# Deeper buffers, sums of the values three steps on, and an expert's transfers in two steps of four

## The chip, the cores and the metric

The kernel runs on one core of one Trainium2 chip. The metric is the device time of one execution in microseconds (us), as the median of the runs. Five engines work side by side, each through its own list of instructions in order, and wait for one another with semaphores: TensorE (PE, matmuls, with weight loads as PEld), VectorE (DVE), ScalarE (ACT), GpSimd (POOL) and SyncE (SP, which here only issues transfers). Transfers run on 16 DMA engines that all issuers share.

## The reference

Two transformer layers on 16 sequences of 112 tokens, width 256, each with a context of 375 rows. Layer A: cross-attention with 8 heads of 64, then a mixture of 8 experts of which each token takes two. Layer B: cross-attention with 16 heads, then a feed-forward part with a convolution and quantised weights. Cut to what matters here:

```python
sim  = einsum('bqhd,bkhd->bhqk', q * SCALE, k)      # keys: 375 context rows + 112 latents = 487
attn = softmax(where(valid, sim, NEG_INF))
out  = einsum('bhqk,bkhd->bqhd', attn, v) @ Wout
x    = x + tanh(g_xattn[0]) * out
# experts: h = silu(x @ w1[e].T) * (x @ w3[e].T);  y = h @ w2[e].T;  8 experts, top 2 by a router
```

All products are made to nearly f32 precision by splitting each operand into two f16 halves (high and low) and adding three products (`PASSES`).

## The kernel before

**Steps and pairs.** The attention work is cut into 192 pairs of heads: 64 pairs in layer A (four of each sequence), then 128 in layer B (eight of each). All engines walk the same list of steps `j` from -9 on, each with its own code for the step. In step `j` PE makes the scores of pair `j`, the queries and keys of pair `j + 2`, the values of pair `j`, and then, in `sum_values(j - 2)`, the product of probabilities and values of pair `j - 2`. A head of a pair is a unit `u = 2 * j + h`.

**The way of one unit.** PE writes the scores; DVE masks them and finds the minimum (`mask_scores`, L1438); ACT takes the exponential (`exp`, L927) and rounds to f16 (`round_probs`, L934) into buffer `u % 4` of `PR`; POOL subtracts to get the low half (`split_probs`, L711); SP issues a DMA transpose (`turn_probs`, L569) of the 112 x 1024 f16 values into buffer `u % 5` of `PT`; PE sums (`sum_values`, L1190: per head 12 matmuls of 64 columns). A buffer of `PR` is free when the transpose of unit `u - 4` has landed, a buffer of `PT` when unit `u - 5` is summed. The values of a pair are in `vN`, two buffers by `j % 2`: ACT rounds pair `j`'s values (`round_v`, L954) in step `j`, after the sum of pair `j - 2`. PE waits in `sum_values` for the values' split, for the transpose, and, in the first unit of eight, for `norm_out` of the group of eight before (L1470), which DVE does in step `4 * g + 6`.

**The experts' weights.** Beside the first steps ACT and DVE turn the f32 weights of the eight experts into f16 halves: three chunks of 512 columns in two steps (`expert_chunks`), so one expert (six chunks) in four steps. ACT issues its plain transfers in `load_weights(j)`, after `round_probs`: for expert `e` three loads of a third (128 partitions x 1024 f32, 512 KB each) from HBM into `raw`, which hold the weights of the expert two before until they are split; and three stores of f16 halves, 512 KB each, back to HBM. In every four steps ACT also loads one context (375 KB, L853), at the head of a step `4 * k + 2`, and spills one turned context (375 KB, L858), at the head of a step `4 * k`. From step 38 on, the tokens of the first six sequences run through the experts (`up`, `down`), with weights and rows that SP loads.

**Order around the change.** Per step ACT does `round_q`, `exp` twice, `round_k`, `round_probs` twice, `load_weights`, `round_v`, context and latents, `round_expert`. The rounding of layer B's weights (`round_l1_chunk`) goes one chunk a step from step 49 on into `W`; chunks 17 and 19 to 23 of `W` are written last.

## Time and profile before

| | |
|---|---|
| runs | 1463.2, 1463.97, 1465.99 us, median 1463.97 |
| profiled execution | 1468.41 us, of which the span from first to last instruction is 1466.7 us |
| mean granted TensorE clock | 0.956 |
| PE, DVE, ACT, POOL busy | 86%, 73%, 66%, 75% of the span |
| DMA | 239.99 MB, mean 164 GB/s |

The span is what the rows are measured in; "busy" is an average over stages with different limits.

### The profile page before, as it was taken

How to read it: one execution, taken by the hardware profiler on the slowest of the kernel's cores; microseconds unless marked ns; L12 is line 12 of the kernel's file. 1: busy time of each engine (PE TensorE's matmuls, PEld its weight loads, DVE VectorE, ACT ScalarE, POOL GpSimd, SP SyncE). 2: the span in 40 equal slices, each digit the busy share in tenths (PEclk: the TensorE clock that was granted, in tenths of full speed). 3: DMA queues.
4: the chain of work that ended last, by engine and by line, in shares of the span. 5: the costliest groups of instructions: out<-in, count | busy, mean ns of one | idle time of the engine just before them, and what ended most of it. 6: DMA issues, size and time to landing. Idle time of an engine off the chain costs nothing.

```text
span 1466.7 us, 45534 instructions
## 1 busy us (share of the span) xinstructions
PE 1256.6 (86%) x16920; PEld 983.7 (67%) x16920; DVE 1066.3 (73%) x2851; ACT 971.8 (66%) x2319; POOL 1094.1 (75%) x1346
## 2 busy tenths in 40 slices
PE   1877788779899988868999999999999999999863
PEld 1555566558777766646888788677777777777652
DVE  5788677966566678775666666778878778888655
ACT  2887778656556666544656465777787877787741
POOL 5887777687677765464777767798888888889763
PEclk9999889989999999998999999999999999999995
DMA  7799998799999968458999999456454545445420
GB/s 252 160 205 192 203 202 169 126 213 236 233 244 269 261 137 200 102 116 198 246 253 247 238 259 224 95 105 111 94 101 99 105 104 100 100 94 103 79 64 7
DMA packets 453500, 239.99 MB, mean 164 GB/s; under 512 B 390320, under 2 KB 424992, under 8 KB 452768
## 3 DMA queue, kind: packets, MB, share of 16 engines
q1 hardware_dynamic: 417912, 178.51, 62.5%
q10 hardware_dynamic: 32296, 51.23, 11.7%
q0 software_dynamic: 3072, 7.34, 1.7%
q8 instruction: 135, 2.21, 0.7%
q14 instruction: 85, 0.70, 0.2%
HBM read 107.78 MB, written 35.50 MB: 98 GB/s over the span
## 4 chain that ended last, share of the span: by engine, by line
PE 52%; POOL 12%; ACT 10%; DMA 7%; DVE 7%; issue 7%; DVEq 2%; ACTq 2%; another core or an unknown queue 0%; SPq 0%; POOLq 0%
PE bank_ring L1171 10%; PE bank_ring L1157 9%; PE bank_ring L1209 8%; PE bank_scores L1131 5%; PE bank_out L1190 5%; DMA probs_turned<-probs 4%; PE bank_x L1272 4%; PE bank_x L1223 4%; POOL probs L711 3%; PE bank_x L1144 3%; ACT scores L927 3%; ACT probs L934 2%; DVE scores L1438 2%; ACTq L1072 2%; POOL moe_rows L730 1%
## 5 line engine op out<-in xcount | busy, mean ns | idle before, releaser
L711 POOL TENSOR_TENSOR probs<-scores,probs 112x487 f16<-112x487 f32 x373 | 414.1, 1127 | 203.9 <-ACT probs L934 199.1
L927 ACT ACTIVATE scores<-scores,score_min 112x487 f32<-112x487 f32 x384 | 265.9, 694 | 159.1 <-DVE score_min L1438 157.0
L1438 DVE CUSTOM_DVE_ANT_0 scores<-bank_scores,mask 112x487 f32<-112x487 f32 x384 | 238.2, 657 | 1.8 <-PE bank_scores L1131 1.3
L934 ACT ACTIVATE probs<-scores 112x487 f16<-112x487 f32 x384 | 214.3, 604 | 32.2 <-DMA probs_turned<-probs 16.5
L1190 PE MATMUL bank_out<-values,probs_turned 128*128 128x64 f16 x4608 | 172.7, 195 | 40.5 <-DMA probs_turned<-probs 21.8
L1171 PE MATMUL bank_ring<-weights,kv_B 128*128 128x128 f16 x3072 | 195.4, 220 | 5.6 <-DVE keys L1455 3.9
L1171 PEld LDWEIGHTS bank_ring<-weights,kv_B 128*128 128x128 f16 x3072 | 184.0, 99 | 15.3 <-DVE keys L1455 5.2
L954 ACT ACTIVATE values<-bank_ring 128x512 f16<-128x512 f32 x192 | 112.3, 585 | 119.5 <-PE bank_out L1190 111.2
L1190 PEld LDWEIGHTS bank_out<-values,probs_turned 128*128 128x128 f16 x4608 | 158.7, 99 | 46.4 <-issue 25.3
L1460 DVE SCALAR_TENSOR_TENSOR values<-bank_ring,values 128x512 f16<-128x512 f32 x192 | 132.2, 688 | 77.3 <-ACT values L954 73.1
L1157 PE MATMUL bank_ring<-kv_B,weights 128*128 128x488 f16 x768 | 180.3, 371 | 0.0
L1131 PE MATMUL bank_scores<-keys,queries 64*112 64x488 f16 x1152 | 164.6, 392 | 4.1 <-DVE score_min L1438 3.7
L1209 PE MATMUL bank_ring<-raw_weights,expert_up 128*128 128x128 f16 x2064 | 131.2, 221 | 13.8 <-issue 13.8
L1209 PEld LDWEIGHTS bank_ring<-raw_weights,expert_up 128*128 128x128 f16 x2064 | 122.9, 99 | 26.0 <-issue 18.4
L1455 DVE SCALAR_TENSOR_TENSOR keys<-bank_ring,keys 128x488 f16<-128x488 f32 x192 | 126.1, 657 | 10.7 <-ACT keys L947 5.3
L947 ACT ACTIVATE keys<-bank_ring 128x488 f16<-128x488 f32 x192 | 106.6, 555 | 4.0 <-PE bank_ring L1157 3.7
L1171 PE MATMUL bank_ring<-weights,kv_A 128*128 128x128 f16 x1536 | 101.9, 226 | 6.6 <-DVE keys L1455 6.6
L1157 PEld LDWEIGHTS bank_ring<-kv_B,weights 128*128 128x128 f16 x768 | 69.4, 99 | 56.2 <-issue 1.7
L1171 PEld LDWEIGHTS bank_ring<-weights,kv_A 128*128 128x128 f16 x1536 | 96.1, 102 | 11.8 <-DVE keys L1455 8.0
L940 ACT ACTIVATE queries<-bank_x 128x112 f16<-128x112 f32 x192 | 49.2, 256 | 75.0 <-PE bank_x L1144 69.4
L1157 PE MATMUL bank_ring<-kv_A,weights 128*128 128x488 f16 x384 | 98.6, 397 | 0.0
L1131 PEld LDWEIGHTS bank_scores<-keys,queries 64*112 64x112 f16 x1152 | 61.1, 129 | 41.3 <-issue 15.0
(236 smaller groups left out, 2446.0 us busy)
## 6 DMA issues: line engine op xcount, KB each, us to landing
expert_up<-experts_up SPq DMA_DIRECT2D x86, 512.0 KB, 5.3
expert_down<-experts_down SPq DMA_DIRECT2D x43, 512.0 KB, 5.7
raw_weights<-in_weights ACTq DMA_DIRECT2D x18, 512.0 KB, 6.7
experts_up<-expert_up ACTq DMA_DIRECT2D x16, 512.0 KB, 4.6
probs_turned<-probs SPq DMA_TRANSPOSE x384
context_turned_B<-kv_B ACTq DMA_DIRECT2D x16, 375.0 KB, 8.0
kv_B<-context_turned_B ACTq DMA_DIRECT2D x16, 375.0 KB, 4.0
moe_results<-moe_result SPq DMA_DIRECT2D x43, 128.0 KB, 5.3
```

Source lines behind the costliest of these rows:

```text
L711: pool.tensor_tensor(PR[:, u % 4, 1, 0:KEYS], S[:, u % 4, 0:KEYS], PR[:, u % 4, 0, 0:KEYS], ALU.subtract).then_inc(probs_split[u % 2], 1)
L927: act_e.activation(S[:, u % 4, 0:KEYS], S[:, u % 4, 0:KEYS], ACT.Exp, bias=rmin[:, u % 4:u % 4 + 1], scale=-1.0, accum_out=rsum[:, g % 2, ...
L934: act_e.activation(PR[:, u % 4, 0, 0:KEYS], S[:, u % 4, 0:KEYS], ACT.Copy).then_inc(probs_ready, 1)
L954: act_e.activation(vN[:, j % 2, 0], bank("v", j)[:].rearrange("p (t d) -> p t d", t=4), ACT.Copy, scale=1 / WSCALE).then_inc(v_hi, 1)
L1131: last = pe.matmul(bS[h][0:TOK, 0:KW], qT[r, j % 2, a, :], kT[r, j % 2, b, :], start=n == 0, stop=n == 2)
L1157: last = pe.matmul(bK[:, 0:KW], w(wk + kb * step, a, 128 * (j % 4), 128), kv[layer][:, n % 2, kb, b, 0:KW], start=i == 0, stop=i == 5)
L1171: last = pe.matmul(bV[:, 128 * t:128 * t + 128], kv[layer][:, n % 2, kb, a, 128 * t:128 * t + 128], w(wv + kb * step, b, 128 * (j % 4), 12 ...
L1190: last = pe.matmul(bO[:, col:col + HD], PT[u % PT_BUFS][:, at:at + 128], vN[:, j % 2, b, t, HD * h:HD * h + HD], start=i == 0, stop=i == 11)
L1209: last = pe.matmul(bH[:, 128 * q:128 * q + 128], eup[:, t % 2, at:at + 128], xT[:, t % 2, KB * c + kb, :], start=k == 0, stop=k == 5)
L1438: dve.tensor_tensor_reduce(out=S[:, u % 4, 0:KEYS], in0=bS[u % 2][0:TOK, 0:KEYS], in1=mask[:, m, 0:KEYS], scale=1.0, scalar=3.0e38, op0=AL ...
L1455: dve.scalar_tensor_tensor(kT[:, j % 2, 1, :], bank("k", j)[:, 0:KW], 1 / WSCALE, kT[:, j % 2, 0, :], ALU.mult, ALU.subtract).then_inc(k_s ...
L1460: dve.scalar_tensor_tensor(vN[:, j % 2, 1].rearrange("p t d -> p (t d)"), bank("v", j)[:], 1 / WSCALE, vN[:, j % 2, 0].rearrange("p t d -> ...
```

## The change

It has these parts.

1. `PT` has 8 buffers, `PR` 6 and `vN` 3 for the first 56 pairs, then 5, 4 and 2 as before. The added ones lie in chunks 17 and 19 to 23 of `W`. `in_turn` makes a table of (buffer, the user before it, how many uses) for every unit or pair. `round_l1_chunk(10)`, the first that writes into one of these chunks, waits for the sum of pair 55.
2. `summed_in(j)`: pairs up to 51 are summed three steps on, except that the last pair of a sequence (`p % 4 == 3`) is still summed two steps on. So a step `4 * k + 1` sums two pairs, a step `4 * k + 2` none. From pair 52 on all are summed two steps on.
3. `expert_loads` and `expert_stores`: counted in fours, loads of the thirds go from steps 0, 1, 3 to steps 1, 1, 2, and stores from 1, 2, 3 to 1, 2, 2. All six plain transfers of a cycle are issued in steps `4 * k + 1` and `4 * k + 2`.
4. Where `split_probs` of the second head goes from POOL to DVE and back (steps 33 to 37 and 73 to 78), the first waits for the split before it instead of for its transpose.
5. DVE sets the pads of the added buffers to zero at the start: four more small `memset`s.

```diff
-PT_BUFS = 5
+LONG_PAIRS = 56
+PT_BUFS, PR_BUFS, V_BUFS = (8, 5), (6, 4), (3, 2)
+def summed_in(j):
+    return [p for p in (j - 3, j - 2) if is_pair(p) and j - p == (3 if p < LONG_PAIRS - 4 and p % 4 < 3 else 2)]
+def in_turn(count, long_count, bufs):
+    places, last, uses = [], {}, {}
+    for i in range(count):
+        b = i % (bufs[0] if i < long_count else bufs[1])
+        uses[b] = uses.get(b, 0) + 1
+        places.append((b, last.get(b), uses[b]))
+        last[b] = i
+    return places
+PT_AT = in_turn(2 * PAIRS, 2 * LONG_PAIRS, PT_BUFS)
+PR_AT = in_turn(2 * PAIRS, 2 * LONG_PAIRS, PR_BUFS)
+V_AT = in_turn(PAIRS, LONG_PAIRS, V_BUFS)
 def expert_loads(j):
-    return [(e, p) for e in range(2, EXPERTS) for p in range(3) if j == 4 * (e - 2) + (4, 5, 7)[p]]
+    return [(e, p) for e in range(2, EXPERTS) for p in range(3) if j == 4 * (e - 2) + (5, 5, 6)[p]]
 def expert_stores(j):
-    return [(e, p) for e in range(EXPERTS) for p in range(3) if j == 4 * e + 5 + p]
+    return [(e, p) for e in range(EXPERTS) for p in range(3) if j == 4 * e + (5, 6, 6)[p]]
...
             def turn_probs(u):
-                if u >= PT_BUFS:
-                    sp.wait_ge(values_summed, u - PT_BUFS + 1)
+                buf, prev, _ = PT_AT[u]
+                if prev is not None:
+                    sp.wait_ge(values_summed, prev + 1)
...
             def round_l1_chunk(c):
                 act_e.wait_ge(l1_loaded[c % len(L1_SLOTS)], 16 * (c // len(L1_SLOTS) + 1))
+                if c == 10:
+                    act_e.wait_ge(values_summed, 2 * LONG_PAIRS)
...
             def round_probs(u):
-                if u >= 4:
-                    act_e.wait_ge(turned[(u - 4) % PT_BUFS], turns_done(u - 4))
+                prev = PR_AT[u][1]
+                if prev is not None:
+                    act_e.wait_ge(turned[PT_AT[prev][0]], turns_done(prev))
...
             def round_v(j):
                 act_e.wait_ge(v_ready, j + 1)
-                if j >= 2:
-                    act_e.wait_ge(values_summed, 2 * (j - 1))
+                prev = V_AT[j][1]
+                if prev is not None:
+                    act_e.wait_ge(values_summed, 2 * prev + 2)
...
                 expert(m[1])
-                if is_pair(j - 2):
-                    sum_values(j - 2)
+                for p in summed_in(j):
+                    sum_values(p)
...
                     if any(j == steps[0] for steps in VECTOR_SPLITS):
-                        dve.wait_ge(turned[(2 * j - 1) % PT_BUFS], turns_done(2 * j - 1))
+                        dve.wait_ge(probs_split[1], j)
                     split_probs(2 * j + 1)
```

## Rows read from the trace of the kernel before

**Rows 1.** The page: busy time by engine, and DMA share in 40 slices.

```profile
PE 1256.6 (86%) x16920; PEld 983.7 (67%) x16920; DVE 1066.3 (73%) x2851; ACT 971.8 (66%) x2319; POOL 1094.1 (75%) x1346
...
DMA  7799998799999968458999999456454545445420
```

**Rows 2.** Four-step stretches: length, PE, PEld, DVE, ACT, POOL busy, PEclk, DMA share, GB/s.

```profile
62.30:91.60 29.30, 21.13 (x278) 15.33 (x279) 24.13 (x60) 24.58 (x57) 24.34 (x28) 0.94 0.97 169
91.60:118.90 27.30, 23.10 (x295) 16.86 (x294) 22.84 (x57) 22.61 (x53) 22.92 (x31) 0.94 1.12 217
118.90:150.60 31.70, 23.92 (x296) 17.47 (x295) 23.02 (x58) 22.99 (x53) 23.03 (x31) 0.89 1.13 191
150.60:180.20 29.60, 23.67 (x295) 17.43 (x295) 22.59 (x58) 22.73 (x53) 22.87 (x31) 0.90 1.13 197
180.20:210.10 29.90, 24.25 (x297) 17.62 (x296) 22.56 (x58) 22.80 (x53) 22.88 (x31) 0.90 1.08 196
...
241.20:266.10 24.90, 20.23 (x283) 14.73 (x282) 22.29 (x63) 20.22 (x48) 21.69 (x29) 1.00 0.85 167
...
424.60:463.70 39.10, 37.59 (x538) 31.68 (x536) 27.02 (x70) 25.43 (x61) 30.09 (x46) 1.00 1.15 268
```

**Rows 3.** The chain that ended last, from 120 us: start, us, what.

```profile
135.42 13.70 DMA probs_turned<-probs
...
150.70 1.40 PE bank_scores L1131 x6
...
158.18 0.76 PE bank_scores L1131 x6
...
159.34 1.24 PE bank_ring L1157 x6
...
182.36 2.26 PE bank_ring L1157 x6
...
196.87 11.70 DMA probs_turned<-probs
```

**Rows 4.** Waits of PE from 39.2 to 210.1 us: total, times, longest.

```profile
PE bank_out L1190 <- DMA probs_turned<-probs: 21.8, 9, 4.2
PE bank_out L1190 <- issue: 4.8, 4, 1.2
```

**Rows 5.** PE in order of time, 60 to 96 us; idle before in brackets.

```profile
61.53 0.52 PE L1190 MATMUL bank_out<-values,probs_turned 128*128 128x64 f16 x12 [0.66 <-DMA probs_turned<-probs]
...
91.10 0.52 PE L1190 MATMUL bank_out<-values,probs_turned 128*128 128x64 f16 x12 [3.36 <-DMA probs_turned<-probs]
```

**Rows 6.** ACT in order of time, 150 to 181 us; idle before in brackets.

```profile
157.92 0.60 ACT L954 ACTIVATE values<-bank_ring 128x512 f16<-128x512 f32 x1 [1.64 <-PE bank_out L1190]
...
166.61 0.70 ACT L927 ACTIVATE scores<-scores,score_min 112x487 f32<-112x487 f32 x1 [0.66 <-DVE score_min L1438]
...
178.73 0.61 ACT L934 ACTIVATE probs<-scores 112x487 f16<-112x487 f32 x1 [3.23 <-DMA probs_turned<-probs]
```

**Rows 7.** DMA queues, 118 to 151 us: packets, MB, share of 16 engines.

```profile
q1 hardware_dynamic: 9528, 2.37, 70.3%
q10 hardware_dynamic: 1792, 4.00, 41.9%
```

**Rows 8.** DMA queue of SP, 596 to 625 us: eight transposes, hardly anything else.

```profile
q1 hardware_dynamic: 7424, 1.84, 29.5%
```

**Rows 9.** Short stretches, columns as in rows 2.

```profile
136.00:148.00 12.00, 5.90 (x84) 4.35 (x84) 8.85 (x20) 7.76 (x18) 7.68 (x9) 0.95 1.33 132
...
131.00:132.30 1.30, 1.30 (x17) 0.69 (x14) 1.30 (x3) 1.22 (x5) 0.80 (x1) 1.00 0.05 13
...
180.00:182.00 2.00, 2.00 (x13) 1.05 (x14) 1.14 (x3) 2.00 (x4) 1.92 (x3) 0.50 1.14 340
```

**Rows 10.** DVE in order of time, 0 to 30 us.

```profile
1.08 0.13 DVE L1378 MEMSET probs_turned<- 128x8 uint32 x5
...
6.58 1.08 DVE L1484 BATCH_NORM_STATS2 bn_stats<-context 125x6 f32<-125x256 f32 x3 [2.11 <-DMA context<-in_ctx]
```

More of the change, by code:

```diff
@@ L349, in build @@
         PR = sb("probs", [TOK, 4, 2, 512], F16)
-        PT = [sb(f"probs_turned_{i}", [128, 8 * TOK + 16], F16) for i in range(PT_BUFS)]
+        PT = [sb(f"probs_turned_{i}", [128, 8 * TOK + 16], F16) for i in range(PT_BUFS[1])]
+        PT += [W[:, 2 * c * CHUNK:2 * c * CHUNK + 8 * TOK + 16] for c in (23, 19, 17)]
+        PR_more = W[0:TOK, 2 * 20 * CHUNK:2 * 22 * CHUNK].rearrange("p (b a c) -> p b a c", b=2, a=2)
+        vN_more = W[:, 2 * 22 * CHUNK:2 * 23 * CHUNK].rearrange("p (a t d) -> p a t d", a=2, t=4)
         mask = sb("mask", [TOK, 2, KEYS + 1], BF16)
@@ L443, in build @@
         probs_ready, probs_split = sem("probs_ready"), [sem("probs_split_0"), sem("probs_split_1")]
-        turned = [sem(f"probs_turned_{i}") for i in range(PT_BUFS)]
+        turned = [sem(f"probs_turned_{i}") for i in range(PT_BUFS[0])]
         values_summed, out_normed, o_hi = sem("values_summed"), sem("out_normed"), sem("o_hi")
@@ L501, in turns_done, with probs, values @@
         def turns_done(u):
-            return 16 * (u // PT_BUFS + 1)
+            return 16 * PT_AT[u][2]
+        def probs(u):
+            b = PR_AT[u][0]
+            return PR[:, b] if b < PR_BUFS[1] else PR_more[:, b - PR_BUFS[1]]
+        def values(j):
+            b = V_AT[j][0]
+            return vN[:, b] if b < V_BUFS[1] else vN_more
         block = stack.enter_context(nc.Block())
@@ L568, in turn_probs @@
                 sp.wait_ge(probs_split[u % 2], u // 2 + 1)
-                sp.dma_start_transpose(PT[u % PT_BUFS][:, 0:8 * TOK].rearrange("p (j q) -> p j q", j=8),
-                                       PR[:, u % 4].rearrange("p a c -> p (a c)"))\
-                    .then_inc(turned[u % PT_BUFS], 16)
+                sp.dma_start_transpose(PT[buf][:, 0:8 * TOK].rearrange("p (j q) -> p j q", j=8),
+                                       probs(u).rearrange("p a c -> p (a c)"))\
+                    .then_inc(turned[buf], 16)
             for j in STEPS:
@@ L710, in split_probs @@
                 pool.wait_ge(probs_ready, u + 1)
-                pool.tensor_tensor(PR[:, u % 4, 1, 0:KEYS], S[:, u % 4, 0:KEYS],
-                                   PR[:, u % 4, 0, 0:KEYS], ALU.subtract).then_inc(probs_split[u % 2], 1)
+                pool.tensor_tensor(probs(u)[:, 1, 0:KEYS], S[:, u % 4, 0:KEYS],
+                                   probs(u)[:, 0, 0:KEYS], ALU.subtract).then_inc(probs_split[u % 2], 1)
             def split_hidden(b, i, half):
@@ L824, in _ @@
                     if any(j == steps[-1] + 1 for steps in VECTOR_SPLITS):
-                        pool.wait_ge(turned[(2 * j - 1) % PT_BUFS], turns_done(2 * j - 1))
+                        pool.wait_ge(probs_split[1], j)
                     split_probs(2 * j + 1)
@@ L931, in round_probs @@
             def round_probs(u):
-                if u >= 4:
-                    act_e.wait_ge(turned[(u - 4) % PT_BUFS], turns_done(u - 4))
-                act_e.activation(PR[:, u % 4, 0, 0:KEYS], S[:, u % 4, 0:KEYS], ACT.Copy).then_inc(probs_ready, 1)
+                prev = PR_AT[u][1]
+                if prev is not None:
+                    act_e.wait_ge(turned[PT_AT[prev][0]], turns_done(prev))
+                act_e.activation(probs(u)[:, 0, 0:KEYS], S[:, u % 4, 0:KEYS], ACT.Copy).then_inc(probs_ready, 1)
             def round_q(j):
@@ L951, in round_v @@
                 act_e.wait_ge(v_ready, j + 1)
-                if j >= 2:
-                    act_e.wait_ge(values_summed, 2 * (j - 1))
-                act_e.activation(vN[:, j % 2, 0], bank("v", j)[:].rearrange("p (t d) -> p t d", t=4), ACT.Copy,
+                prev = V_AT[j][1]
+                if prev is not None:
+                    act_e.wait_ge(values_summed, 2 * prev + 2)
+                act_e.activation(values(j)[:, 0], bank("v", j)[:].rearrange("p (t d) -> p t d", t=4), ACT.Copy,
                                  scale=1 / WSCALE).then_inc(v_hi, 1)
@@ L1183, in sum_values @@
                         pe.wait_ge(out_normed, u // 8)
-                    pe.wait_ge(turned[u % PT_BUFS], turns_done(u))
+                    pe.wait_ge(turned[PT_AT[u][0]], turns_done(u))
                     i = 0
@@ L1189, in sum_values @@
                             at = TOK * (4 * a + t)
-                            last = pe.matmul(bO[:, col:col + HD], PT[u % PT_BUFS][:, at:at + 128],
-                                             vN[:, j % 2, b, t, HD * h:HD * h + HD], start=i == 0, stop=i == 11)
+                            last = pe.matmul(bO[:, col:col + HD], PT[PT_AT[u][0]][:, at:at + 128],
+                                             values(j)[:, b, t, HD * h:HD * h + HD], start=i == 0, stop=i == 11)
                             i += 1
@@ L1376, in _ @@
             dve.memset(PR[:, :, :, KEYS:512], 0.0)
+            dve.memset(PR_more[:, :, :, KEYS:512], 0.0)
             for t in PT:
@@ L1444, in split_probs @@
                 dve.wait_ge(probs_ready, u + 1)
[L1445 removed]
+                dve.tensor_tensor(probs(u)[:, 1, 0:KEYS], S[:, u % 4, 0:KEYS], probs(u)[:, 0, 0:KEYS],
                                   ALU.subtract).then_inc(probs_split[u % 2], 1)
```

5 lines of the change are left out of this document (2 added, 3 removed).

## The prediction

> **What bounds the kernel now.** I read the page first, for the whole: PE is busy 86% of the span, and the DMA engines stand near full in the first half and near half in the second [rows 1]. The change touches layer A up to pair 55, so I cut that part into stretches of four steps, one sequence each, and read busy time, clock and DMA share in each [rows 2]. Three kinds of stretch show. From 62 to 210 us (steps 4 to 23) four steps take 27.3 to 31.7 us while no engine is busy for more than 24.6, and the DMA share is 0.97 to 1.13 (it passes 1 since packets of two queues overlap). From 241 us, where the experts' loads are over, four steps take 24.9 us. In the stage with the experts' products, as at 424 us, PE is busy 37.6 of 39.1 us at full clock.
>
> Then the chain of waits [rows 3]. From step 4 to 23 it runs on PE alone, broken once in four steps by a DMA transpose that took 11.7 to 13.7 us from issue to landing (three such from 135 us). PE waited 21.8 us for transposes between 39 and 210 us [rows 4]; these waits stand in steps 3, 7, 11, 15, 19 and 23, always for pair `4k + 1`; those of steps 3 and 7 are 0.7 and 3.4 us [rows 5]. The same list over the whole run gives the same line, so no later stage has such a wait. So 21.8 us is the prize, plus what follows from it: after each wait the granted clock is 0.50, the lower of the two levels (1.2 of 2.4 GHz), where before it was 1.00 [rows 9], and the same six score matmuls take 1.40 in place of 0.76 us, the six key matmuls 2.26 in place of 1.24 us [rows 3]. These two alone are 1.66 us a wait.
>
> **The change, part by part.**
>
> *Sums three steps on.* Pair `4k + 1` is now due one step, some 6 us, later. The longest waits were 4.2 us for one head, some 4.5 for the pair, so at today's landing times each would go: 21.8 us for six waits, 1.66 us of clock for each of the last five, 8.3 us. One more wait goes: PE waited four times up to 1.2 us for `norm_out` before the first sum of a group (4.8 us in all, [rows 4]); that sum moves one step behind `norm_out`. PE's own limit on this change is therefore about 21.8 + 8.3 + 4.8 = 34.9 us.
>
> *ACT.* ACT waited 3.2 us per cycle for a transpose to free a buffer of `PR` [rows 6]; with six buffers it waits for one a pair older, so this goes too. It is not on the chain by itself, but it held the next `exp` and the transfers behind it. ACT's other waits in such a cycle are 1.64 us for the sum before `round_v` and 0.66 us for masked scores [rows 6]. The first stays, since the third buffer of `vN` comes with a sum one step later, except in one step of four. ACT is busy 22.7 to 23.0 us per four steps [rows 2]; with 2.3 to 2.6 us of such waits it can't do a cycle under about 25.3 us. DVE and POOL, at 22.6 to 23.0, say the same, and the cycle at 241 us took 24.9. I take 25.3 us as the engines' floor.
>
> *DMA.* This is where I doubt that the whole prize comes. Four steps move 5.8 MB (197 GB/s x 29.6 us). Eight transposes with hardly anything beside them take 29.5% of 29 us, 8.6 us of the DMA engines [rows 8]. In the stretch from 118 to 151 us the same queue moved 2.37 MB, which at that rate is 11.1 us, but took 70.3% of 33 us, 23.2 us; the plain queue took 13.8 us for 4.00 MB [rows 7]. So transposes beside plain transfers cost twice their time, and from 136 to 148 us the two together moved 132 GB/s [rows 9]. The DMA engines idle only while PE's wait starves the issuers: 131.0 to 132.3 us at a share of 0.05 [rows 9]; I estimate 1.0 us of such idle time per cycle from this one of 1.3. If the transfers stay as inefficient, a cycle can't fall under 29.6 (the mean of the four from 91 to 210 us, [rows 2]) - 1.0 = 28.6 us, whatever the buffers.
>
> *Grouping the six transfers.* Before, every pair's transposes meet a plain transfer: ACT issues them in all four steps. After, 3.1 MB plus the context (0.38 MB) go out within about 6 us, and the transposes of two pairs of four (`4k + 1`, `4k + 2`) meet them, both with three steps to land. Pairs `4k + 3` and `4k` meet only the spill and the tail of the group. What this saves isn't shown by any row. Below: nothing, 28.6 us a cycle. Above: all transposes clean, 8.6 + 13.8 = 22.4 us, and then the engines' floor of 25.3 counts. I take the middle, 27.0 us, since about half of the transposes still meet plain transfers.
>
> A rule of the Trainium skill speaks against any saving here: "DMA: Bandwidth & Descriptors", section Queues, rings and completion order, has each DMA engine take turns between the queues it has work for, packet by packet; by that alone the order of transfers moves no work, and a cycle stays at 28.6 us. The share of 70.3% against 29.5% says that taking turns isn't all that happens beside transposes.
>
> *The sum.* By stretches of [rows 2]: 27.3 to 27.0 saves 0.3; 31.7, 29.6 and 29.9 to 27.0 save 10.2; the one at 62 us, with a DMA share under 1, loses its wait of 3.4 us; the short wait in step 3 gives 0.7. Together 14.6 us. The waits for `norm_out` and the clock are inside these cycles and aren't added. Against it I set 1.5 us for steps 24 to 36, where pair `4k + 3` is now the only one with two steps and meets stores gathered just before it. Net 13.1 us.
>
> *Edits costed at nothing.* The steps from 38 to 55 are bound by PE (37.6 of 39.1 us busy), and the same matmuls stay; if that cover were gone, earlier transposes could only help. A sum moved within a cycle is 0.7 us of PE work in another place. The wait in `round_l1_chunk(10)` is for a sum made two steps before. Dropping POOL's or DVE's wait for a transpose at steps 33, 38, 73 and 79 takes away a wait that isn't on the chain; with the cover gone it would be worth at most a landing, 3 us each. Four more memsets, like the five that took 0.13 us together, lie ahead of a context load that DVE waits for 2.1 us [rows 10]; uncovered they would cost some 0.1 to 0.5 us. `load_weights` issues the same transfers, none with a new wait that ACT meets: each load waits for a split at least a step old.
>
> The profiled execution took 1468.4 us, 1.7 more than its span, so after the change it should show 1455.3, with a span of 1453.6. The median of the runs is 4.4 us lower, so 1463.97 - 13.1 = 1450.9 us; I say 1451.
>
> **The rivals.**
>
> *The engines' floor is reached.* If grouping makes the transposes nearly clean, four cycles of 25.3 us save 2.0 + 6.4 + 4.3 + 4.6 = 17.3, with the 4.1 of steps 3 and 7 and none lost: 21.4 us, 1442.6 us. For it: 22.4 us of clean DMA work in a cycle. Against: two pairs still meet 3.5 MB.
>
> *Grouping saves nothing.* Cycles of 28.6: 3.1 + 1.0 + 1.3 + 4.1 = 9.5, less 1.5: 8.0 us, 1456.0 us. This is also what the skill's rule gives.
>
> *The wait moves and stays.* Pair `4k + 3` has its two steps still, and its transposes stand behind those of pair `4k + 2` in SP's queue, which now meet the group. If PE waits there as long as it did for `4k + 1`, the cycle stays near 29.6 us, and the time near 1463, within 3 us.
>
> *Slower.* The same place at a higher price. The group, a context and four transposes are 3.15 + 0.38 + 0.92 = 4.45 MB; the other four transposes take 4.3 us clean. A cycle of 29.6 us leaves 25.3 us for the 4.45 MB, 176 GB/s. Under that rate the change is slower than before. The stretch at 136 us had 132 GB/s, whole cycles have 191 to 217. At 160 GB/s a cycle takes 32.1 us, 2.5 longer, over six cycles with loads 15 us: 1479 us.
>
> **How the numbers follow.** A measurement of this kernel tells about 0.2% (3 us) from no change. Chances: the middle case with its neighbours (1446 to 1455) 0.42; the floor 0.12; grouping saves nothing or part of the wait stays (1455 to 1461) 0.19; the wait moves whole 0.14; slower 0.13. That makes faster 0.73, same 0.14, slower 0.13. The likeliest case's own range is 1445 to 1457. For 8 in 10 the range runs from the engines' floor, 1441, to no change and a little over, 1466.
>
> **What would show it.** Right: PE waits for transposes before step 24 fall from 21.8 us to under 8; four steps there take 26 to 28 us; the clock in these stretches rises from 0.90; the DMA share stays near 1 with more GB/s. Steps from 24 on keep their lengths within 1 us each. Grouping right: the share of SP's queue for the same MB falls. Wrong: waits of PE for transposes in steps `4k + 1` from 5 on (the wait moved), or ACT or DVE late in the cycle with PE waiting for masked scores or keys (the floor lies higher than 25.3), or a slower start of steps 24 to 37.

## The result and the profile after

The changed kernel takes 1473.87 us, the median of 7 runs (1470.09 to 1482.97), against 1463.97 us of 7 runs before. The ratio is 1.0087, with a 95% interval from 1.0054 to 1.0120: the change makes the kernel slower, by 9.9 us going by the medians and by some 13 us going by the ratio. I had said 1451.

The profiled execution took 1477.87 us with a span of 1476.1, 9.4 more than before. Single executions differ more than I knew when I predicted. The kernel before ran from 1446 to 1478 us in the comparisons below, and its first profile, at 1468.4, lies high. So I profiled each kernel twice; the second profile of the kernel before took 1452.7 us, that of the changed kernel 1467.6. Where two numbers stand for these two kernels, as 147.8 / 138.1, they are of the first and the second profile.

The page, PE and the DMA engines in 40 slices, against [rows 1]:

```profile
PE 1265.4 (86%) x16920; PEld 991.4 (67%) x16920; DVE 1060.0 (72%) x2855; ACT 970.0 (66%) x2319; POOL 1093.7 (74%) x1346
...
DMA  8699999799999979358999999446354555445420
```

PE is busy 8.8 us longer with the same 16920 matmuls. That is the clock, as the stretches of four steps show. They start at step 4 and have the columns of [rows 2]: length, PE, PEld, DVE, ACT, POOL, PEclk, DMA share, GB/s.

```profile
63.00:89.30 26.30, 22.15 (x278) 16.00 (x278) 21.29 (x57) 23.40 (x56) 22.29 (x27) 0.87 0.82 160
89.30:121.30 32.00, 26.08 (x296) 18.37 (x296) 20.92 (x55) 21.71 (x50) 22.67 (x30) 0.84 1.17 175
121.30:151.60 30.30, 24.91 (x297) 18.18 (x296) 23.60 (x63) 24.42 (x58) 21.55 (x30) 0.89 1.19 184
151.60:183.80 32.20, 25.29 (x297) 18.03 (x296) 20.52 (x56) 21.18 (x49) 22.47 (x30) 0.84 1.19 200
183.80:213.20 29.40, 24.58 (x297) 17.74 (x296) 23.90 (x64) 24.46 (x58) 22.24 (x30) 0.88 1.19 200
...
244.00:268.90 24.90, 20.28 (x283) 14.65 (x282) 22.55 (x65) 20.22 (x49) 22.71 (x30) 1.00 1.00 170
431.30:470.00 38.70, 37.25 (x537) 31.62 (x534) 26.96 (x70) 25.30 (x61) 29.95 (x46) 1.00 1.15 274
```

The first stretch is 3 us shorter than its counterpart, as I expected. It is also the one in which the loads have hardly begun. The four loaded ones take 31.0 us on average, where they took 29.6 before and I had forecast 27.0. Their DMA share rose to 1.17 to 1.19, and yet fewer bytes move in a microsecond: 190 GB/s over steps 8 to 23 against 200. The DMA engines don't idle meanwhile. In the packets' records, cut into slices of a quarter microsecond, SP's or ACT's queue fills more than 10% of the 16 engines in every slice of steps 8 to 23 of the first profile, and in all but 1.25 us of the second; in the kernel before 4 us are left empty. The clock is lower, not higher. The two stretches at the end are as before.

PE's waits from 40.2 to 213.2 us, against [rows 4]:

```profile
PE bank_out L1229 <- DMA probs_turned<-probs: 6.8, 2, 5.3
PE bank_x L1183 <- DVE router_logits L1764: 5.2, 3, 2.4
PE bank_x L1295 <- DVE moe_in_f L1761: 5.2, 3, 2.4
PE bank_out L1229 <- DMA probs_turned<-weights: 3.9, 2, 3.7
...
PE bank_out L1229 <- DMA weights<-probs: 1.3, 1, 1.3
```

(The added buffers lie in the tile `weights`, so a transpose that uses one carries that name.) The waits for transposes did fall, from 21.8 us to 12.0 (13.1 to 9.0 in the second profiles). But they fell behind a third step and not because the transposes came sooner. The chain, against [rows 3], has three transposes that took 16 to 21 us from issue to landing, where before they took 12 to 14:

```profile
82.24 16.48 DMA probs_turned<-weights
...
143.39 21.02 DMA probs_turned<-probs
...
202.27 19.23 DMA probs_turned<-probs
```

The second of them ends at 164.4 us. It releases PE, against [rows 5], and ACT, against [rows 6], at once:

```profile
164.46 0.82 PE L1229 MATMUL bank_out<-values,probs_turned 128*128 128x64 f16 x12 [5.32 <-DMA probs_turned<-probs]
```

```profile
ACT probs L972 <- DMA probs_turned<-probs: 7.0, 1, 7.0
```

The wait of ACT for a buffer of `PR` is back, longer than the 3.2 us of [rows 6], with six buffers in place of four. It comes less often: over steps 4 to 23 these waits are 10.4 / 7.3 us, where they were 15.7 / 6.1. PE's clock behind it is the lower of its levels, as in [rows 9]:

```profile
164.40:166.40 2.00, 1.95 (x19) 1.44 (x21) 0.41 (x1) 1.64 (x4) 1.25 (x2) 0.50 1.25 210
```

The DMA queues from 121 to 151 us, against [rows 7], and SP's from 602 to 632 us, where there is hardly anything else, against [rows 8]:

```profile
q1 hardware_dynamic: 6713, 1.67, 63.5%
q10 hardware_dynamic: 1749, 3.88, 53.9%
```

```profile
q1 hardware_dynamic: 7568, 1.97, 29.4%
```

The plain queue takes 53.9% of 30 us, 16.2 us, for 3.88 MB, where it took 13.8 us for 4.00 MB. The transposes take 11.4 us per MB here; before they took 9.8, and clean ones take 4.5. Per byte the packets of both kinds took longer. This is not yet engine time that is lost: it is the sum of the packets' durations, and packets of one queue overlap in the records, as the 126.9% of SP's queue alone shows further down.

After step 24 there is more. Steps 24 to 43 take 179.9 / 180.0 us, where they took 174.6 / 173.4. Steps 44 to 55 give 1 to 2 us of it back, with 117.8 / 118.5 against 120.0 / 119.6.

### The profile page after: what moved, and what is told of

The parts are those of the page before. It is cut to its first block, busy times and chain, and to the rows that moved or that the text cites. A ratio compares the mean times of both kernels' runs of the same rounds, so it can differ in the third digit from the quotient of the medians.

```text
span 1476.1 us, 45538 instructions
## 1 busy us (share of the span) xinstructions
PE 1265.4 (86%) x16920; PEld 991.4 (67%) x16920; DVE 1060.0 (72%) x2855; ACT 970.0 (66%) x2319; POOL 1093.7 (74%) x1346
## 4 chain that ended last, share of the span: by engine, by line
PE 47%; ACT 12%; POOL 10%; issue 9%; DVE 9%; DMA 8%; ACTq 3%; DVEq 2%; SPq 1%; POOLq 0%
PE bank_ring L1210 8%; PE bank_ring L1196 8%; PE bank_ring L1248 8%; PE bank_out L1229 5%; PE bank_scores L1170 5%; ACT scores L964 4%; PE bank_x L1311 3%; PE bank_x L1262 3%; DMA probs_turned<-probs 3%; PE bank_x L1183 2%; POOL probs L746 2%; DVE scores L1478 2%; ACT probs L972 2%; ACTq L1111 2%; ACT keys L985 2%
## 5 line engine op out<-in xcount | busy, mean ns | idle before, releaser
L746 POOL TENSOR_TENSOR probs<-scores,probs 112x487 f16<-112x487 f32 x338 | 373.0, 1121 | 181.5 <-ACT probs L972 179.0
L972 ACT ACTIVATE probs<-scores 112x487 f16<-112x487 f32 x348 | 193.8, 604 | 25.9 <-DMA probs_turned<-probs 11.7
L1210 PEld LDWEIGHTS bank_ring<-weights,kv_B 128*128 128x128 f16 x3072 | 184.5, 99 | 12.7 <-DVE keys L1495 4.1
L1196 PE MATMUL bank_ring<-kv_B,weights 128*128 128x488 f16 x768 | 184.0, 377 | 0.0
L1500 DVE SCALAR_TENSOR_TENSOR values<-bank_ring,values 128x512 f16<-128x512 f32 x174 | 119.8, 688 | 75.5 <-ACT values L993 71.9
L1229 PE MATMUL bank_out<-values,probs_turned 128*128 128x64 f16 x3828 | 140.7, 194 | 20.3 <-issue 10.3
L993 ACT ACTIVATE values<-bank_ring 128x512 f16<-128x512 f32 x174 | 101.4, 583 | 85.3 <-PE bank_out L1229 84.3
L1229 PEld LDWEIGHTS bank_out<-values,probs_turned 128*128 128x128 f16 x3828 | 130.3, 99 | 23.8 <-issue 12.5
L1248 PEld LDWEIGHTS bank_ring<-raw_weights,expert_up 128*128 128x128 f16 x2064 | 124.8, 100 | 25.3 <-issue 17.3
L1210 PE MATMUL bank_ring<-weights,kv_A 128*128 128x128 f16 x1536 | 105.5, 230 | 7.1 <-DVE keys L1495 7.0
L1210 PEld LDWEIGHTS bank_ring<-weights,kv_A 128*128 128x128 f16 x1536 | 99.5, 104 | 13.0 <-DVE keys L1495 9.0
```

The source lines that it names most:

```text
L746: pool.tensor_tensor(probs(u)[:, 1, 0:KEYS], S[:, u % 4, 0:KEYS], probs(u)[:, 0, 0:KEYS], ALU.subtract).then_inc(probs_split[u % 2], 1)
L972: act_e.activation(probs(u)[:, 0, 0:KEYS], S[:, u % 4, 0:KEYS], ACT.Copy).then_inc(probs_ready, 1)
L1196: last = pe.matmul(bK[:, 0:KW], w(wk + kb * step, a, 128 * (j % 4), 128), kv[layer][:, n % 2, kb, b, 0:KW], start=i == 0, stop=i == 5)
L1210: last = pe.matmul(bV[:, 128 * t:128 * t + 128], kv[layer][:, n % 2, kb, a, 128 * t:128 * t + 128], w(wv + kb * step, b, 128 * (j % 4), 12 ...
L1229: last = pe.matmul(bO[:, col:col + HD], PT[PT_AT[u][0]][:, at:at + 128], values(j)[:, b, t, HD * h:HD * h + HD], start=i == 0, stop=i == 11)
L1248: last = pe.matmul(bH[:, 128 * q:128 * q + 128], eup[:, t % 2, at:at + 128], xT[:, t % 2, KB * c + kb, :], start=k == 0, stop=k == 5)
```

## The experiments

Ratios are to the kernel before, run beside each on the same chip (its medians there were 1458.4, 1459.6 and 1459.6 us, and 1463.97 beside the changed kernel). The table has what the profiles show of each: the length of steps 4 to 23, of 24 to 43 and of 24 to 55, the DMA share and rate over steps 8 to 23, and "both", the part of steps 8 to 23 in which transposes and plain transfers are on the DMA engines together. I worked out "both" from the trace's records of packets: it is the sum of the slices of a quarter microsecond in which SP's queue and ACT's queue each fill more than 10% of the 16 engines.

| kernel | ratio (95%) | steps 4–23 | 24–43 | 24–55 | share, GB/s | both |
|---|---|---|---|---|---|---|
| before | 1 | 147.8 / 138.1 | 174.6 / 173.4 | 294.6 / 293.0 | 1.11, 200 / 1.11, 212 | 41 / 44 |
| changed | 1.0087 (1.0054–1.0120) | 150.2 / 144.2 | 179.9 / 180.0 | 297.7 / 298.6 | 1.18, 190 / 1.16, 196 | 74 / 65 |
| e1 changed, not grouped | 0.9987 (0.9951–1.0023) | 132.2 | 177.6 | 300.9 | 1.14, 220 | 40 |
| e2 before, grouped | 1.0329 (1.0280–1.0377) | 182.9 | 176.5 | 296.8 | 0.87, 159 | 60 |
| e3 deep buffers alone | 0.9968 (0.9935–1.0001) | 136.8 | 168.9 | 295.8 | 1.10, 213 | 38 |
| e4 changed, thin loads | 0.9966 (0.9932–1.0001) | 133.5 | 178.2 | 298.3 | 0.86, 173 | 21 |
| e5 changed, sums two on | 1.0285 (1.0229–1.0340) | 184.0 | 170.9 | 294.7 | 0.96, 162 | 70 |
| e6 transposes held back | 1.0103 (1.0067–1.0140) | 148.3 | 179.1 | 297.7 | 1.14, 189 | 74 |
| e7 before, thin loads | 0.9889 (0.9834–0.9944) | 130.0 | 169.3 | 286.9 | 0.92, 171 | 23 |
| e8 three steps on early only, not grouped | 0.9937 (0.9908–0.9967) | 139.8 | 168.0 | 293.3 | 1.10, 211 | 46 |
| e9 only loads grouped | 1.0176 (1.0126–1.0226) | 162.8 | 186.4 | 307.5 | 1.18, 169 | 100 |
| e10 only stores grouped | 1.0047 (1.0013–1.0081) | 144.7 | 180.1 | 298.2 | 1.12, 197 | 56 |

**e1: the change without the grouping.**

```
-    ... if j == 4 * (e - 2) + (5, 5, 6)[p]]
+    ... if j == 4 * (e - 2) + (4, 5, 7)[p]]
-    ... if j == 4 * e + (5, 6, 6)[p]]
+    ... if j == 4 * e + 5 + p]
```

> The changed kernel with the six plain transfers of a cycle back in their old steps (loads 0, 1, 3, stores 1, 2, 3), all else as changed. Theory G (grouping makes transposes and plain transfers share the DMA engines for longer, 16 to 21 us a cycle against 9 to 11 before): cycles of steps 8 to 23 fall from 30 to 32 us to about 27 to 28, mixed time falls back near 10 us, and the kernel is 8 to 14 us faster than before, near 1455. Theory B (the deeper buffers themselves let more transposes meet the plain transfers, whatever the steps): cycles stay at 30 to 32 us and the kernel is within 3 us of the changed one, near 1473. If ScalarE's running ahead is what delays the last scatters at step 38, that part (about 4 us) stays here in either case.

Its ratio is 0.9987: all that the change loses, it loses by the grouping. The same buffers and sums with it are 1.0% slower, some 15 us. Theory G holds in the cycles, which fall to 26.8 us on average, but only half in the time: 1455.7 us is near the 1455 that it names, yet the kernel before took 1458.4 beside it, so the gain of 8 to 14 us isn't there. Steps 8 to 23:

```profile
88.80:195.90 107.10, 89.54 (x1179) 66.81 (x1178) 89.42 (x229) 89.37 (x208) 93.85 (x119) 0.94 1.14 220
```

The same transfers in other steps reach 220 GB/s in place of 190, and the clock 0.94 in place of 0.86. Since the DMA engines hardly idle in either kernel (0.25 us are empty here) and the bytes are the same, the order alone changes what they move in a microsecond. PE waits for transposes only twice in steps 4 to 23, both times in step 9, for the two heads of pair 7 (`4k + 3`):

```profile
PE bank_out L1229 <- DMA weights<-probs: 7.1, 2, 5.6
```

**e2: the grouping alone, in the kernel before.** The same two lines changed the other way, with five, four and two buffers and the sums two steps on.

> The kernel before with only the six plain transfers gathered in two steps; old buffers, sums two steps on. Theory G: four transposes meet 3.5 MB of plain transfers with only two steps to land, so TensorE waits more than before: 5 to 15 us slower than before, near 1474. Theory B: grouping is harmless, within 3 us of before.

It takes 1503.48 us, 3.3% more, three times the most that I had set for theory G. PE's waits from 62.1 to 244.0 us:

```profile
PE bank_out L1190 <- DMA probs_turned<-probs: 48.7, 10, 10.4
PE bank_out L1190 <- issue: 8.2, 4, 2.1
```

With 21.1 / 12.7 us before in steps 4 to 23, the grouping adds 28 to 36 us of waiting for transposes. The mean clock over these steps falls from 0.91 to 0.82.

**e3: the deep buffers alone.** The sums are two steps on and the transfers in their old steps.

```
-    ... j - p == (3 if p < LONG_PAIRS - 4 and p % 4 < 3 else 2)]
+    ... j - p == 2]
```

> Deeper buffers only: sums two steps on for all pairs, transfers in their old steps. Theory G: TensorE's waits for pair 4k+1 stay (21.8 us before) but ScalarE's 3.2 us per cycle for a buffer of PR go, so 0 to 4 us faster than before. Theory B: as slow as the changed kernel, 5 to 10 us slower than before.

The ratio is 0.9968 (0.9935 to 1.0001), within the 0 to 4 us of theory G and just short of a difference that can be told. PE still waits 13 us for transposes in steps 4 to 23 (21.1 / 12.7 in the kernel before), ACT no longer for a buffer of `PR`.

**e4: the changed kernel with thin loads.** Each load of a third brings 128 columns in place of 1024, for experts 2 to 7, so seven eighths of these loads are left out; what is left and the stores stay grouped.

```
-    act_e.dma_start(raw[..., (2 * p + 2) * CHUNK], weights_in[:, at:at + 2 * CHUNK])
+    act_e.dma_start(raw[..., 2 * p * CHUNK + 128], weights_in[:, at:at + 128])
```

> The changed kernel with each load of a third of an expert's weights (experts 2 to 7) cut from 1024 to 128 columns, so 1.4 of 3.1 MB of a cycle's plain transfers are left out; the experts' products then use other weights, with the same work. If the DMA engines set the length of steps 4 to 27, the cycles fall to the engines' floor (I reckoned 25.3 us) and the kernel ends 20 to 35 us under the changed one, 1440 to 1453. If engines' own couplings set it, the cycles stay above 28 us and it gains under 10 us.

No wait for a transpose is left, yet the time falls only to 1455.11 us, 2 us above the range that I had set for DMA as the limit. PE's waits from 60 to 190 us:

```profile
PE bank_x L1183 <- POOL mask L735: 6.0, 3, 3.1
PE bank_x L1183 <- DVE router_logits L1764: 5.3, 3, 2.6
PE bank_x L1295 <- DVE moe_in_f L1761: 5.2, 2, 2.6
```

So this is close to the engines' own floor in the changed order (stores and contexts are still moved): 133.5 us for twenty steps, 26.7 a cycle.

**e5: the changed kernel with all sums two steps on.** The edit of e3, with the grouping kept.

> The changed kernel with its deep buffers and its grouped loads and stores, but with every sum two steps after its pair, as in the kernel before. Grouping alone, with the old buffers and sums two steps on, took 1503 us; the changed kernel, with both, 1474. Theory B (the deep buffers rescue most of it: what grouping delays is then only the pair's own transposes, and not ACT's and SP's queue behind them): 1474 to 1485 us, PE's waits for transposes between 10 and 30 us over steps 3 to 23. Theory S (the third step is what covers the transposes that meet the group, since they take 12 to 21 us from issue to landing in the changed kernel): 1490 us or more, with PE waits for transposes of 35 to 50 us. In both, steps 24 to 40 take about 131 us as in the two kernels with sums two steps on, and not 135 to 136, if it is the sums' place that lengthens those steps.

It takes 1500.84 us (1.0285), hardly less than e2. So theory S holds: with the grouping the buffers do nearly nothing, and the third step makes up for most of it. PE's waits for transposes, of 49 us in steps 4 to 23:

```profile
PE bank_out L1229 <- DMA probs_turned<-probs: 27.3, 6, 6.5
PE bank_out L1229 <- DMA probs_turned<-weights: 21.9, 4, 7.6
```

**e6: transposes held back until loads have landed.** Two waits more in SP's queue.

```
+    for e in range(2, EXPERTS):
+        for p, step in ((1, 6), (2, 7)):
+            if j == 4 * (e - 2) + step:
+                sp.wait_ge(third_loaded[e % 2][p], 16 * (e // 2))
```

> The changed kernel with two waits more in SP's queue for each expert from 2 to 7: the transposes of step 4k + 2 are issued only after the load of the second third has landed, those of step 4k + 3 only after the load of the last third has. So the transposes meet fewer plain transfers, and nothing else is changed. Theory M (a transpose beside a plain transfer costs the DMA engines about twice its time, so that what is mixed is lost): the time in which both queues are active falls from 16 to 21 us a cycle, DMA shares fall under 1.1, and the time comes at 1460 to 1468 us, 6 us or more under the changed kernel. Rival Q (the engines only take turns and no work is lost; the transposes are late because they queue behind or beside the group): transposes start later and land no earlier, the time is 1474 us or more, with PE waits for transposes of 20 us or more.

The ratio is 1.0103, within the interval of the changed kernel's own. The time fits neither theory's range (1460 to 1468, and 1474 or more). And the profile shows that the experiment missed its aim: the time in which both queues are active is 74 us, as without the waits, since the transposes of pair `4k + 1`, which meet the whole group, aren't held back by them, nor do they keep the stores away. So it can't tell one theory from the other.

**e7: the kernel before with thin loads.** The edit of e4 in the old order.

> The kernel before with the loads of the experts' thirds cut from 1024 to 128 columns (experts 2 to 7; the output is computed with other weights). The changed kernel with the same cut took 1455 us, with no PE wait for a transpose and cycles of 24.0 to 29.4 us (mean 26.7) in steps 4 to 20. If buffers and later sums are worth something once the plain transfers are gone, this one is slower than that. Theory F (the sums' place three steps on costs DVE and PE some microseconds of its own, and the old order has no waits left once transposes are clean): 1445 to 1453 us, cycles of 24 to 26 us in steps 4 to 20. Rival (the old buffers bind also without plain transfers): 1455 to 1462 us, with PE or ACT waits for transposes left in these cycles.

1440.43 us, 5 us under the range of theory F. The rival fails, and what theory F said of the cycles and waits holds: the cycles in steps 4 to 23 take 26.0 us on average, and no wait for a transpose is left but a short one. PE's waits from 60 to 190 us:

```profile
PE bank_x L1144 <- POOL mask L700: 7.7, 3, 3.8
PE bank_x L1144 <- DVE router_logits L1724: 6.4, 3, 2.3
...
PE bank_out L1190 <- DMA probs_turned<-probs: 0.3, 1, 0.3
```

Two things follow. Seven eighths of the loads cost the kernel before 1.1% (16 us; 19 by the medians), so that is about all there was to win by hiding transposes. And the changed order with the same thin loads (e4) is 0.8% slower than the old order, by 3.5 us in steps 4 to 23 and 11.4 in steps 24 to 55: even if the grouping had made all transposes clean, I estimate from e4 that the change as made would have come to about 1455 us.

**e8: deep buffers, transfers in their old steps, three steps on only for pairs before 20.**

```
-    ... j - p == (3 if p < LONG_PAIRS - 4 and p % 4 < 3 else 2)]
+    ... j - p == (3 if p < 20 and p % 4 < 3 else 2)]
```

> The deep buffers of the changed kernel, loads and stores in their old steps, and the sums three steps on only for pairs before 20 (three of four); from pair 20 all sums are two steps on again. With sums three on up to pair 51 this kernel took 1455.7 us (ratio 0.9987), with sums two on throughout 1455.1 (0.9968). Theory C (a third step saves time where transposes meet loads, and costs 4 us in steps 24 to 40, which took 133 to 137 us with sums three on and 130 to 132 with sums two on in all profiles so far): steps 24 to 40 take 130 to 132 us, the ratio is 0.993 to 0.996. Rival D (what is lost in steps 24 to 40 isn't from the sums' place, or the third step costs as much before step 24 as it saves): ratio 0.997 to 1.000.

1451.22 us, the ratio 0.9937 (0.9908 to 0.9967). This version beats both kernels. It is the time that I had forecast for the changed one, though against 1459.6 us beside it the gain is 8 to 9 us and not 13. Steps 24 to 43 take 168.0 us, as in e3, and not 177 to 180 as in the kernels with the late third step. In steps 24 to 39, of which I had given numbers, it took 128.4 us, under what theory C asked for. Much of this comes back in steps 44 to 55, which take 125.3 us (126.9 in e3) against 117.8 to 123.3 with the late third step; why, I can't say. That e8 is better than e3, the buffers alone, isn't shown: the intervals overlap. Those of e8 and e1 overlap by a hair too.

**e9 and e10: the loads grouped alone, and the stores.** Each undoes the other's line.

> The changed kernel with only the loads grouped (steps 5, 5, 6 of four); the stores are in their old steps (5, 6, 7). The changed kernel with both grouped has the ratio 1.009, with neither 0.9987. If the loads' place is what delays the transposes (two of three loads move, and both now stand in the steps in which pairs 4k + 1 and 4k + 2 are transposed): ratio 1.006 to 1.010. If each transfer put into the group counts alike (three moved, two of them loads): 1.005. If the store is it: 0.998 to 1.002.

> The changed kernel with only the stores grouped (one store moved, from step 7 to step 6 of four); the loads are in their old steps (4, 5, 7). If the loads' place is what delays the transposes: ratio 0.998 to 1.002, as with neither grouped (0.9987). If each moved transfer counts alike: 1.002. If the store is it: 1.006 to 1.010.

The loads alone give 1.0176, worse than both together, and the stores alone 1.0047, more than nothing. Neither number was among those that I had set, and the two don't add. With the loads grouped and the last store in its old step 7, no step of the four is left without a plain transfer behind the group: transposes and plain transfers share the engines for 100 of 138 us. That moving the store to step 6 frees step 7, and so lowers the price from 1.9% to 1.0% above nothing grouped (e1), I read from this; no run moved the store to yet another step.

```profile
88.40:226.20 137.80, 101.41 (x1182) 72.75 (x1178) 92.90 (x237) 93.81 (x212) 90.92 (x121) 0.85 1.18 169
```

A share of 1.18 and 169 GB/s: no slice is empty here either, and less is moved than in any other kernel of which that holds.

**The second profiles.**

> The kernel before, unchanged, for a second profile of it. Its runs differ by up to 20 us, and its first profile (1468 us) lies on the high side of them. A second one shows how far a single profile's cycles can be trusted: if the cycles of steps 4 to 24 repeat within 1 us each, differences of 2 us between profiles are the kernels' own; if they differ by 2 to 4 us, only sums over several cycles can be compared.

> The changed kernel, unchanged, for a second profile. The kernel before took 147.8 and 138.1 us for steps 4 to 23 in two profiles, and 130.7 and 131.2 for steps 24 to 39. If the change costs what its first profile shows, steps 4 to 23 take 145 to 155 us here too, with a share of the DMA engines of 1.15 to 1.2, and steps 24 to 39 take 134 to 137 us. If the first profile was a slow execution, steps 4 to 23 come under 142 us.

The kernel before took 27.9, 25.0, 26.7, 28.9 and 29.6 us for its five cycles from step 4, against 29.3, 27.4, 31.7, 29.6 and 29.9. Only the last two come back within 1 us, and the sum is 9.7 us less. The changed kernel took 144.2 us for the five, just under the 145 to 155 that I expected but over the 142 that would have made the first profile an outlier, 136.6 for steps 24 to 39, within what I expected, and 180.0 for steps 24 to 43, as at first. A single cycle of one profile is no evidence for a few microseconds. Even twenty steps of one profile can be off by as much: e1 and e8, which differ there only in when pairs 20 and 21 are summed, took 132.2 and 139.8 us for steps 4 to 23. What many kernels show alike is better.

**What mixing costs.** Three stretches of the changed kernel: SP's queue alone, ACT's queue alone, and both. First the stretches, with the columns of [rows 2]:

```profile
134.30:138.30 4.00, 2.44 (x56) 2.11 (x54) 3.06 (x10) 3.21 (x9) 1.99 (x4) 1.00 1.30 167
199.80:204.80 5.00, 3.79 (x44) 2.60 (x40) 3.77 (x11) 3.48 (x10) 4.76 (x7) 1.00 0.99 286
...
145.80:156.30 10.50, 8.51 (x87) 5.78 (x85) 8.92 (x25) 9.71 (x23) 7.87 (x10) 0.84 1.32 153
```

Then the queues of each: packets, MB and share, in the order of the stretches.

```profile
q1 hardware_dynamic: 2513, 0.63, 126.9%
...
q10 hardware_dynamic: 377, 1.41, 95.3%
...
q1 hardware_dynamic: 1893, 0.47, 72.5%
q10 hardware_dynamic: 580, 1.12, 59.2%
```

Alone, transposes take 4.00 us for 0.63 MB and plain transfers 5.00 us for 1.41 MB. At these rates the 0.47 and 1.12 MB of the last stretch would take 3.0 + 4.0 = 7.0 us, one after the other. Together they took 10.5. In e9, from 116.9 to 136.4 us:

```profile
q1 hardware_dynamic: 3200, 0.80, 80.0%
q10 hardware_dynamic: 1116, 2.27, 44.8%
```

One after the other 5.1 + 8.0 = 13.1 us at the rates of the changed kernel; together 19.5. I chose these stretches for being long. Over all slices of steps 8 to 23 in the first profile of the changed kernel, mixed ones moved 52 GB/s of transposes and 121 GB/s of plain data. Unmixed ones moved about 165 GB/s with transposes (147 to 204 in the kernels with full loads) and 280 with plain data (244 to 308). So 52/165 + 121/280 = 0.75 of the time would have done, and a quarter of each mixed microsecond is lost; with the changed kernel's own unmixed rates, 155 and 252 GB/s, it is 52/155 + 121/252 = 0.82, a loss of a fifth.

The size of the loss hangs on the yardstick. By each kernel's own unmixed rates it is 0.14 to 0.24 in the kernels with full loads; for e9, with 40 and 119 GB/s mixed, it is a quarter by its own 146 and 247, and a third by 165 and 280. With a limit of 20% in place of 10% for a queue to count as active it is 0.06 and 0.18 in the two profiles of the changed kernel. That there is a loss, the rates in e1 and the changed kernel show without it.

Does this price explain the times? In part. The changed kernel mixes for 74 / 65 us, the kernel before for 41 / 44. The 27 us more, at 0.25, are 7 us; steps 8 to 23 took 121.9 us on average of the two profiles, against 114.4, 7.5 more. But these two differ in their buffers and sums as well. Against e1, from which the changed kernel differs in the grouping alone, the 29 us of mixed time more are 7 us too, and the steps took 14.8 us more (121.9 against 107.1). A second part is in the slices in which only plain transfers are active: they moved 309 GB/s in e1 and 247 and 261 in the changed kernel, which on 25 to 30 us is some 5 us. Why they are slower, no run tells, and e1 has one profile, 5.6 us under its median. In e9 the 100 mixed us at a third are 33 us, against 10 in the kernel before: 23 us more, and steps 8 to 23 took 137.8, 23.4 more; against e1 they took 30.7 more, and at e9's own rates the price is 24 us against 8. So mixing is one part of what grouping costs, perhaps half, and its size is an estimate. The order of the kernels with deep buffers and three steps is that of their mixed time: e1 (40 us, 0.9987), e10 (56, 1.0047), changed (74 / 65, 1.0087), e9 (100, 1.0176). The intervals of e1 and e10, and those of e10 and the changed kernel, overlap; the others are apart.

## Why the prediction was wrong, by its steps

**What bounds the kernel.** Right in kind. The stage is one of transposes and loads, and at 16 us (e7) the prize was near my net sum of 13.1. I wrote that the DMA share passes 1 because packets of two queues overlap; the 126.9% of SP's queue alone shows that packets of the transposes' own queue do, without a second one. The prize wasn't PE's waits of 21.8 us plus their clock: the second profile of the kernel before shows 12.7 us of such waits in steps 4 to 23, so part of what I read as the kernel's was one execution's.

**Sums three steps on.** The waits of pair `4k + 1` were to go "at today's landing times", and in e1, with these, all in steps 4 to 23 did: the 7.1 us in two waits that are left are for pair 7, and steps 4 to 23 took 132.2 us, 10.8 less than the mean of the two profiles before. The waits for `norm_out` (4.8 us, "issue" in [rows 4]) are gone from the changed kernel's list. The third step is worth much where transposes are late (e5 against the changed kernel, 2%). What I took for free was the third step in the stage behind: I had costed steps 24 to 36 at 1.5 us, for stores before pair `4k + 3`. Steps 24 to 43 take 168.0 to 170.9 us with deep buffers and two steps (e3, e8, e5), and 177.6 to 180.1 with three (e1, e4, e6, e10, both profiles of the changed kernel; 186.4 in e9): 9 to 10 us. Part of it is only shifted: over steps 24 to 55 it is 293.3 to 295.8 us against 297.7 to 300.9, 4 us between the means, of which the sum of one pair that slips behind step 24 is about 1. e8 shows that it goes with the sums' place. By which wait isn't settled. PE's waits there are longer by a microsecond or two in several places (for DVE's `moe_in_f`, for expert products, for pair `4k + 3`'s transposes), with no single one that holds most of it.

**ACT.** Wrong in the changed kernel: the wait for a buffer of `PR` is 7.0 us once where 3.2 went, behind a transpose that took 21 us. In e1 and e3 it did go.

**The engines' floor.** I had 25.3 us a cycle from ACT's busy time and the cycle at 241 us. With thin loads the cycles take 26.0 us in the old order and 26.7 in the new one, so the term was mis-sized by 1 us a cycle; the waits for DVE's `router_logits` and POOL's `mask` that make it up were hidden behind the transposes. The rival of 1442.6 us was never to be had with this order.

**DMA, four cycles at 28.6 us "if the transfers stay as inefficient".** They didn't stay so, in either direction. e1, at 220 GB/s, averages 26.8 us over steps 8 to 23. The two times that I set against each other, 23.2 us of transposes beside plain transfers and 11.1 clean, were sums of packets' durations, and these grow without any plain transfer: 8.1 us per MB for a burst of transposes alone (from 134.3 us), against 4.7 in [rows 8]. So "twice their time" isn't the price of the plain transfers, and 8.6 + 13.8 = 22.4 us was too low for a cycle of clean transfers. At the unmixed rates of 165 and 280 GB/s the 7.7 and 15.5 MB of steps 8 to 23 need 102 us, by estimate 25.6 a cycle, even if none are mixed: hardly less than the 26.8 that e1 reached with the old spread.

**Grouping: the step that failed.** I wrote that it saves, and took "the middle, 27.0 us, since about half of the transposes still meet plain transfers". The four cycles took 31.0 and 30.0 us on average in the two profiles, and 26.8 in e1 without the grouping; it costs 15 us where I had it save. The bounds were wrong too: I put the lower one at nothing, as if regrouping could only reduce the mixing. I counted which pairs meet a plain transfer. What I left out is for how long both queues are active (16 to 19 us a cycle, against 10 to 11 before and in e1). As I read it, and no run isolates it, four transposes and 3.5 MB issued within 6 us slow each other down, stay in flight for 15 to 20 us, and reach the pairs that should have been clean. The row that could have told me was in front of me, 132 GB/s from 136 to 148 us in [rows 9], the stretch of the old order that is most like a group. I used it for a rival at 0.13 only.

The Trainium skill's rule, in "DMA: Bandwidth & Descriptors", section Queues, rings and completion order, is that the engines take turns packet by packet. By it alone the order moves no work, and I had 1456.0 us from that. The runs here don't agree with that conclusion of mine: at the same bytes the cycles take from 26.8 us (e1) to 34.5 (e9), with at most 0.25 us of empty slices in all four cycles of either.

**The rivals.** The one that held is "slower". Its place was right (the group with the transposes of pairs `4k + 1` and `4k + 2`), and its condition, a mixed rate under 176 GB/s, is met, if barely: 173 GB/s over the mixed slices of the first profile, 153 in the stretch above. Its price of 15 us is near the 15 that e1 shows, but it stood against the kernel before, to which the grouped cycles lost 1.4 / 2.4 us each, where I had 2.5 for this rival; that over the whole the loss comes to 10 to 13 us is in part luck, since a third of it came behind step 24. The wait didn't move whole to pair `4k + 3`: in the changed kernel the longest two (3.7 us in step 8, 5.3 in step 16) were still for pair `4k + 1`, in spite of the third step. In e1 the two that are left do stand where this rival had them.

**Edits costed at nothing.** e3, with all the buffers, the two swapped waits and the extra memsets, has a ratio of 0.9968, so together they cost nothing that can be told. Steps 44 to 55 take 1 to 2 us less than before.

**The numbers.** By the means of the two profiles of each kernel, the span grew by 12.2 us: 4.3 in steps 4 to 23, where I had forecast 13.9 less (so 18 of the 25 us that I was off lie here), 4.4 in steps 24 to 55, where I had 1.5, and 3.6 before step 4 and behind step 55 together, which single profiles can't tell from nothing. 1473.9 us is outside my range of 1441 to 1466. The chance for slower, 0.13, hung on one rate; the one row that I had of such a stretch, 132 GB/s, spoke for it, and I gave whole cycles more weight.

## What to carry to other kernels

Don't gather bulk transfers beside DMA transposes: here it cost 1.0% with deep buffers and 3.3% without. Count for how long both are in flight, not how many transposes meet one; here some 0.14 to 0.33 of that time was lost, by estimate and by the yardstick taken. Before moving transfers together, look for the densest stretch that the trace already has and price the new order by its rate. A wait removed by an extra step of delay should have that delay only where the wait is (steps 24 to 55 take 293.3 us in e8 and 300.9 in e1; in the whole time, 1451 and 1456 us, the two are just short of being told apart), and more than one profile should be read before a wait of a few microseconds is taken for the kernel's.

## What the runs showed of the hardware

Transposes and plain transfers in flight together moved less than one after the other: 10.5 us for what takes 7.0 at the rates of either alone, and in e9 19.5 for 13.1. The packets of each kind took longer: by the sum of their durations over 16 engines, transposes alone took 8.1 us per MB (126.9% of 4.00 us for 0.63 MB), mixed 16.2; plain transfers 3.4 us per MB alone and 5.6 mixed. Whether it is the packets' turns, a shared port or the memory that does it, no run tells. That the order of the same transfers alone changes the rate is shown, by e1 against the changed kernel (220 and 190 / 196 GB/s over steps 8 to 23, with the engines hardly idle in either). That it is the mixing that does so is argued from the order of e1, e10, the changed kernel and e9, and from the rates: the experiment that was to force the two apart (e6) left them together.
